# A linear-attention layer on one core: order of the first key bias products, token statistics kept in PSUM, the last query products split around the spread of the key maxima, and a transposition moved into the second state

## The reference

```
xn = layernorm(x) * ln_w + ln_b
q = softmax(xn @ Wq + bq, per head over 64 features)
k = softmax(xn @ Wk + bk + (1 - mask) * -1e6, over the 2048 tokens)
v = (xn @ Wv + bv) * mask
att = sum over tokens of k^T v          (per head, 64 x 64)
y = q @ att
h = layernorm(y) * (1 + scale) + shift  (scale, shift from silu(cond) @ W_emb + b_emb)
out = x + silu(h) @ W_out + b_out
```

## Time and profile before

| | |
|---|---|
| median of three runs | 477.64 us |
| the profiled execution | 476.57 us |
| its span (first to last instruction) | 474.8 us |
| DVE busy | 360.9 us (76%) |
| ACT busy | 263.8 us (56%) |
| POOL busy | 137.6 us (29%) |
| granted clock of PE | 1.00 in nearly all slices |

### The profile page before, as it was taken

How to read it: one execution, slowest core, us unless ns; L and a number is a source line. 1 busy time by engine, 2 the same in 40 slices (tenths; PEclk the granted TensorE clock), 3 DMA queues, 4 the chain that set the end, 5 groups by cost and what they waited for, 6 DMA issues and landing times.

```text
span 474.8 us, 7355 instructions
## 1 busy us (share of the span) xinstructions
PE 458.6 (97%) x2490; PEld 370.4 (78%) x2490; DVE 360.9 (76%) x877; ACT 263.8 (56%) x488; POOL 137.6 (29%) x152
## 2 busy tenths in 40 slices
PE   4999999999999999999999999999999999999997
PEld 2677776886788878888888888888768868888876
DVE  5879976775977956979678667677798628898963
ACT  4633332321887523347555665556789913778882
POOL 0413311121200000104223223333211133676675
PEclk9999999999999999999999999999999999999999
DMA  7966210113132200110213211121322041243222
GB/s 252 365 204 225 110 45 2 45 43 111 50 128 89 90 32 14 46 44 1 72 41 126 92 50 68 66 89 46 133 86 71 0 145 57 90 126 129 100 91 88
DMA packets 23190, 43.50 MB, mean 92 GB/s; under 512 B 1961, under 2 KB 2289, under 8 KB 23153
## 3 DMA queue, kind: packets, MB, share of 16 engines
q1 hardware_dynamic: 22592, 41.98, 25.8%
q10 hardware_dynamic: 560, 1.05, 0.6%
HBM read 34.64 MB, written 8.39 MB: 91 GB/s over the span
## 4 chain that ended last, share of the span: by engine, by line
PE 78%; DVE 10%; issue 4%; POOL 4%; ACT 1%; DMA 1%; POOLq 0%; ACTq 0%; DVEq 0%
PE ps L1211 20%; PE ps L1213 20%; PE ps L1212 20%; PE ps L1216 8%; PE ps L1395 4%; POOL x_in L635 2%; PE ps L1317 2%; DVE ek_lo L850 1%; PE ps L1270 1%; POOL zT_lo L628 1%; DMA y<-in_L_cond_Wk_dram 1%; DVE kf L845 1%; DVE kf L909 1%; DVE res L969 1%; PE ps L1373 1%
## 5 line engine op out<-in xcount | busy, mean ns | idle before, releaser
L619 POOL TENSOR_TENSOR qs<-qs,qmax 128x512 f32<-128x512 f32 x32 | 35.6, 1113 | 172.9 <-DVE qmax L814 172.9
L1211 PE MATMUL ps<-wk_hi,zT_hi 128*128 128x512 f32 x124 | 51.2, 413 | 2.2 <-DVE kf L795 2.2
L1211 PE MATMUL ps<-ek_hi,zm_hi 128*128 128x512 f32 x128 | 50.7, 396 | 2.0 <-DVE ek_lo L850 1.3
L1211 PE MATMUL ps<-wq_hi,zT_hi 128*128 128x512 f32 x128 | 51.7, 404 | 0.0
L1213 PE MATMUL ps<-wq_hi,zT_lo 128*128 128x512 f32 x128 | 50.2, 392 | 0.0
L1212 PE MATMUL ps<-wq_lo,zT_hi 128*128 128x512 f32 x128 | 49.9, 390 | 0.0
L1212 PE MATMUL ps<-ek_lo,zm_hi 128*128 128x512 f32 x128 | 49.9, 390 | 0.0
L1213 PE MATMUL ps<-ek_hi,zm_lo 128*128 128x512 f32 x128 | 49.9, 390 | 0.0
L338 ACT ACTIVATE zT_hi<-ps 128x512 fp32r<-128x512 f32 x32 | 19.1, 596 | 54.6 <-PE ps L1216 54.6
L1213 PE MATMUL ps<-wk_hi,zT_lo 128*128 128x512 f32 x124 | 48.7, 393 | 0.0
L1212 PE MATMUL ps<-wk_lo,zT_hi 128*128 128x512 f32 x124 | 48.4, 390 | 0.0
(11 more groups left out here) (243 smaller groups left out, 1176.8 us busy)
## 6 DMA issues: line engine op xcount, KB each, us to landing
x_in<-in_x_dram SPq DMA_DIRECT2D x35, 512.0 KB, 3.5
res<-in_x_dram SPq DMA_DIRECT2D x24, 256.0 KB, 2.9
out_dram<-res SPq DMA_DIRECT2D x24, 256.0 KB, 2.0
out_dram<-x_in SPq DMA_DIRECT2D x7, 256.0 KB, 2.0
y<-in_L_cond_Wk_dram ACTq DMA_DIRECT2D x2, 512.0 KB, 5.3
kf<-in_L_cond_Wq_dram SPq DMA_DIRECT2D x1, 1024.0 KB, 5.2
eq<-in_L_cond_W_out_dram SPq DMA_DIRECT2D x1, 1024.0 KB, 8.3
wv_mod<-in_L_cond_Wv_dram SPq DMA_DIRECT2D x1, 1024.0 KB, 10.5
```

Of the source, the lines that this page charges most:

```text
L619: pool.tensor_tensor(q_heads, q_heads, qmax[:, n % 2, :].unsqueeze(2).broadcast_to([P, H, DH]), ALU.subtract).then_inc(s["q_shift"], 1)
L1211: pe.matmul(o, a[0], bb[0], start=start, stop=False)
```

## The change

Nothing that is computed changes. The edits:

1. `key_bias(1)` moves from before the first transpositions to after both first key products.
2. On SP, the load of token tiles 4 and 5 goes ahead of the two broadcast bias loads and of the wait for Wq.
3. The statistics' small values of chunks 2, 3 and 4 of the first batch lie in PSUM too (bank `YB`, columns 128 on; chunk 1 stays in `QB`). `y`, `x_r` and `x_shift` stay in SBUF.
4. First state: `product_q(0, 14)` is issued as two blocks, the spread of the maxima, two blocks. DVE's order at that place is rewritten.
5. Second state: `product_q(1, 15)` is issued as one block, the spread, three blocks; `turn_y(HT + 1)` moves from ahead of the state's first product to behind it; on POOL, `add_bias(HT - 1)` goes ahead of `q_shift(1, 15)`.

```diff
-        xst_ps = in_psum(xst, 128)
+        xst_ps = [in_psum(xst, bank, 128) for bank in (QB, YB)]
...
             load_x(0, 0, 2)
+            load_x(0, 0, 4)
             spread(bk, bk_all[:], "bk_in")
             spread(bq, bq_all[:], "bq_in")
             sp.wait_ge(s["wq_in"], 16)
-            load_x(0, 0, 4)
...
                 if t == T - 1:
                     h_low(HT - 1)
+                    add_bias(HT - 1)
                 q_shift(1, t)
-            add_bias(HT - 1)
...
-                if b == 0 and c == 1:
-                    return xst_ps
+                if b == 0 and c:
+
+                    return xst_ps[min(c, 2) - 1]
...
             keys_top(0)
+            k_less_max(0, 0)
+            k_less_max(0, 1)
+            zm_low(0, 0)
             q_add(0, T - 2)
-            k_less_max(0, 0)
-            zm_low(0, 0)
-            k_less_max(0, 1)
+            ek_low(0, 0)
             q_top(0, T - 2)
-            ek_low(0, 0)
-            q_add(0, T - 1)
             zm_low(0, 1)
             ek_low(0, 1)
+            q_add(0, T - 1)
...
-            def product_q(b, n):
+            def product_q(b, n, blocks=range(NB)):
...
-                last.then_inc(s["q_ps"], 1)
+                if NB - 1 in blocks:
+                    last.then_inc(s["q_ps"], 1)
...
             key_bias(0)
-            key_bias(1)
             turn_z(0, 0)
             turn_z(0, 1)
             product_k(0, 0)
             product_k(0, 1)
             pe.wait_ge(s["vec_in"], 5 * 16)
             turn(ps[:, YB + 1, 0:ROWS - FIRST], vec_rows).then_inc(s["vec_ps"], 1)
+            key_bias(1)
...
-            product_q(0, T - 2)
+            product_q(0, T - 2, range(2))
             spread_kmax(0)
+            product_q(0, T - 2, range(2, NB))
...
             turn_kmax(1)
             turn_y(HT)
+            product_q(1, T - 1, range(1))
             spread_kmax(1)
-            product_q(1, T - 1)
+            product_q(1, T - 1, range(1, NB))
             product_out(HT - 1)
-            turn_y(HT + 1)
             for n in range(T):
                 product_g(1, n)
+                if n == 0:
+                    turn_y(HT + 1)
```

More of the change, by code:

```diff
@@ L127, in cond_linear_attention, with in_psum @@
         xst, yst = stat_tiles("xst"), [stat_tiles("yst0"), stat_tiles("yst1")]
-        def in_psum(st, at):
-            mv = ps[:, QB, at:at + 2 * NT].rearrange("p (t k) -> p t k", k=2)
-            v, bits, a, b = (ps[:, QB, at + 2 * NT + NT * k:at + 3 * NT + NT * k] for k in range(4))
+        def in_psum(st, bank, at):
+            mv = ps[:, bank, at:at + 2 * NT].rearrange("p (t k) -> p t k", k=2)
+            v, bits, a, b = (ps[:, bank, at + 2 * NT + NT * k:at + 3 * NT + NT * k] for k in range(4))
             return {"raw": st["raw"], "mv": mv, "v": v, "bits": bits.bitcast(U32), "y": st["y"], "a": a, "b": b}
-        yst_ps = [in_psum(yst[k], 64 * k) for k in range(2)]
-        xst_ps = in_psum(xst, 128)
+        yst_ps = [in_psum(yst[k], QB, 64 * k) for k in range(2)]
+        xst_ps = [in_psum(xst, bank, 128) for bank in (QB, YB)]
         x_r, x_shift = sb("x_r", [P, T]), sb("x_shift", [P, T])
@@ L1261, in product_q @@
                     pe.wait_ge(s["x_norm"], 2)
-                for f in range(NB):
+                for f in blocks:
                     if m == 0:
```

## The result

The changed kernel took 473.05 us (median of four runs, 472.80 to 474.07), the kernel before 477.38 in the same comparison (four runs, 477.07 to 477.81): a ratio of 0.9913, 95% interval 0.9895 to 0.9931. The forecast was 472.8. The profiled executions are 473.26 against 476.57, spans 471.5 against 474.8, so 3.3 us less by the profiles and 4.3 by the medians. Single runs of one kernel differ: over all comparisons of this document the kernel before took from 475.99 to 479.03. What can be followed from row to row is the profile's 3.3.

A forecast was written before the change was run, and what follows sets the result against it. PE was taken as the bound, busy 458.6 of 474.8 us, leaving 16.2 us idle to win from. Terms 0.1 + 1.9 + 0.9 + 1.9 = 4.8 us gave 477.64 - 4.8 = 472.8, own range 471.8 to 473.8, 8-in-10 range 471.1 to 475.4.

The forecast's parts named there:

- All four places: Where PE stands still: first 21 us, 46 to 48 us, start of the first state, start of the second.
- The three terms behind the start: Gains forecast for chunk 2's statistics (1.9 us), the first state (0.9) and the second state (1.9).
- The start: Up to the first query product: turns 1.1 us earlier, moved passes cost 1.0 later; net gain 0.1 us.
- the rival of the slow pace: At the start, PE's slow pace lasts longer: 4.8 - 2.0 = 2.8 us gained, 474.8; chance 8%.
- The earlier load: Tiles 4 and 5 before two bias loads: statistics end by 19.7 instead of 21.01, leaving PE's own queue as limit.
- The statistics: Chunk 2, near 41 to 48 us: two tiny DVE instructions no longer wait out POOL; 1.9 us gained.
- The first state: At its start: earlier spread and subtraction bring tile 0's ek_lo before the queries end; 0.9 us gained.
- The second state: At its start: the turn waits for nothing and DVE's output tile comes 2.1 us earlier; 1.9 us gained.
- The rival of the statistics not getting free of POOL: Chunk 2's statistics stay held because y and x_r stay in SBUF: 2.9 us gained, 474.7; chance 6%.
- that of the starts of the states giving nothing: At both states, shifted POOL operations hold the low parts; 0.1 + 1.9 is left, 475.6; chance 12%.
- The slower one: At both states' starts POOL holds DVE for its operations' full length, adding 6.1 us: 481.7; chance 4%.
- all the idle time goes: At all four places: 0.9, 1.9, 1.2 and 2.4, together 6.4 us gained, 471.2; chance 13%.

The follow-up runs named there:

- e8_semb: Changed kernel with DVE's two small embedding-condition instructions (semb_t) one tile later, behind tile 4's key and query sums; 0.9913 against the kernel before.
- e5_keybias_only: Kernel before with key_bias(1) moved behind the first two key products and nothing else; 1.0003 against the kernel before.
- e4_keybias_back: Changed kernel with key_bias(1) put back ahead of the first transpositions, all else as changed; 0.9915 against the kernel before.
- e1_stats: Kernel before with only the small statistics values of chunks 2 to 4 put in PSUM; 0.9968 against the kernel before.
- e2_state0: Kernel before with only the first state's edits: product_q(0, 14) in two parts around the spread, DVE's order rewritten; 0.9994 against the kernel before.
- e3_state1: Kernel before with only the second state's edits: last query product split, turn_y(13) behind the first state product, POOL's bias addition moved; 0.9966 against the kernel before.
- e11_state1_no_bias: Kernel before with the second state's PE edits, but POOL's bias addition left behind its subtraction; 1.0004 against the kernel before.
- e7_order: Changed kernel with DVE's second query addition (tile 15) ahead of the low part of tile 1's exponentials; 0.9906 against the kernel before.
- e6_warm: Changed kernel with 18 unused transpositions of the identity on PE while it waits for its first data; 0.9913 against the kernel before.

## Why the prediction was right, term by term

The forecast of 472.8 lies 0.25 from the median and inside its own range. All four places were the right ones and the untouched stretches stayed within 0.03 us. Of the stalls named for removal, the 0.63 and the 0.3 and 0.91 at the states went, and the 1.22 of the key sum shrank to 0.27.

That the sum came so close is in part luck, because errors cancel. The three terms behind the start were forecast at 4.7 and brought 3.49 in the trace, 1.2 too much. The medians differ by 4.33 all the same, so about 0.8 must have come from the start, where the forecast had 0.1. The pair of profiled executions doesn't show it (-0.21), but the other runs do, by an estimate: take from the time of each run the 1.79 us around the span and what its kernel's profile has from the first query product to the end. Left is the time to the first query product. It is 22.06 us on average (standard error 0.07) in the 127 runs of the six programs without the earlier load of tiles 4 and 5, and 21.34 (0.16) in the 22 runs of the four programs that have it and no warm-up.

- *The start*, 0.1 forecast, -0.21 measured. The step that failed is the pace. ACT's split came 1.11 earlier, as worked out (9.83 against 10.94), and the moved passes cost 0.86 later (2.84 for six against 1.98 for four), less than the 1.0 charged. That would be 0.25 won. But the first key product, at the lower level until about 13, gave back 0.45: the second one starts at 14.48 against 15.14, only 0.66 earlier. 1.11 - 0.45 - 0.86 = -0.20, the measured -0.21 up to rounding. This is the rival of the slow pace, which was given 8% at a cost of up to 2.0; here it cost 0.45, enough to eat the gain. It is not a fixed price of the edit: with the same start and no gap ahead of the turns PE rose near 10.6 in `e8_semb`. `e5_keybias_only` (1.0003) and, more weakly, `e4_keybias_back` (0.9915) say that the edit is worth nothing that the timing can tell. The page of the Trainium skill cited for that rival, "TensorE: Matmul & The Clock Gate", Part 1, had the clock rise only after sustained activity. The traces agree as far as they go: in all thirteen the first pass over Wk was slow and PE was at work when its pace rose. They don't tell how much work is enough.
- *The earlier load*, costed at nothing, since without it the statistics ended "exactly when PE is ready". That held for the one execution that was profiled. The first query product waits for `x_shift` in four of the six profiles without the load (0.45, 0.24, 0.40 and 0.45 us in `e1_stats`, `e2_state0`, `e3_state1` and `e11_state1_no_bias`) and in none of the seven with it; in the changed kernel the statistics end at 18.96, 2.3 before that product. By the estimate above the load is worth about 0.7 us, the term that the sum left out. By itself it wasn't run, so this is likely and not shown.
- *The statistics*, 1.9 forecast, 1.44 measured, 1.45 alone. The rule by which it was argued held: one input in PSUM is enough. What the sum left out is the next instruction with two inputs in SBUF: `semb_t` at 43.48 used to run after POOL was done, and now runs under it: 0.60 where 0.17 is usual, 0.43 given back. `e8_semb`, which moves it away, has 1.96 there.
- *The first state*, 0.9 forecast, 0.37 measured, 0.33 alone. The cost was named ("POOL's shift of tile 14 now falls on two DVE instructions") but not charged: `ek_low(0, 1)` took 1.53 for 0.68 and held the query addition and all of DVE's work behind it. The low part of tile 2, which was to come 1.2 to 1.8 earlier, ends only 0.37 earlier, counted from the last key product. `e7_order` shortens that `ek_low` to 0.93, puts the addition ahead of it, and wins 0.96 in all.
- *The second state*, 1.9 forecast, 1.68 measured, 1.70 alone. The output tile on DVE did come 2.16 earlier, counted from the transpositions of the maxima (2.1 forecast), and the low part behind it lost 0.44 under POOL's shift (1.12 for 0.68), where 0.2 had been taken off; what is left, 1.7, goes on unchanged to the fourth product. The masked tile's 0.92 had slack. What the prediction had wrong is the share of the parts: it gave the turn alone 0.9 as its lower bound. `e11_state1_no_bias` shows 0.0 for turn and split without POOL's new order.

The rival of the statistics not getting free of POOL is refuted by `e1_stats`, and that of the starts of the states giving nothing by `e3_state1` and the rows of `e2_state0`. The slower one is refuted too: DVE is held by POOL at both states, but for 0.85, 0.39 and 0.44 us in new places, not 6.1. That all the idle time goes is refuted by the stalls that are left, 0.27, 0.28, 0.22 and 1.11.

## What to carry to other kernels

When a stall under another engine goes, the sum should go on to the next instruction of the same kind: here the one that moved into the place of a removed collision took back 0.5 us at the statistics, 0.6 at the first state and 0.4 at the second. Where two waits end at the same resource, a release of one is worth nothing until the other goes too; here one line on POOL decided over 1.7 us that a bigger edit on PE seemed to bring. Work of PE moved out of its slow first microseconds is paid for later (0.86 here), and where a gap opened in its place, PE also came to its upper pace late. And a wait that just isn't there in the one execution that was profiled can be there in most others: the load that was costed at nothing is the example.

## What the runs showed of the hardware that was not expected

- The landing of the first half of Wk lay anywhere from 5.77 to 8.06 us in the thirteen profiled executions, and the first query product came 13.7 to 15.8 us behind it, at 20.23 to 23.10. From there to the end executions hardly differ: 453.71 us in both kernels with the old program there (before and `e5_keybias_only`), and 450.20, 450.01 and 450.24 in three with the new one (the changed kernel, `e4_keybias_back`, `e6_warm`).
- PE's pace rose at another time in each execution, with the same instructions ahead of it: in the five with the old start (before, `e1_stats`, `e2_state0`, `e3_state1`, `e11_state1_no_bias`) near 10.5, 10.4, 11.2, 13.0 and 12.7 us. With one key bias product moved away it rose near 10.6 and 12.9 where PE worked on without a gap (`e8_semb`, `e7_order`), and near 13.0 and 14.4 where it had a gap of 0.87 or 0.51 ahead of the turns, although Wk had landed earliest there (5.77 and 6.23, in the changed kernel and `e5_keybias_only`). That the gap is the cause is likely and not shown.
- Eighteen transpositions ahead of the first pass, 0.21 apart, never reached the upper pace. Behind an idle time of 0.48 the next two passes took 1.61, behind 0.83 they took 2.05; four behind 1.99 took 3.65, where four at the upper level take 1.98 and four without any warm-up took 3.48 to 3.75.
- POOL's work also holds a TENSOR_SCALAR with a single SBUF tile as input: 1.04 for 0.17 at 16 elements, 0.92 for 0.53 at 512. And it goes the other way: POOL's own operation took 1.49 for 1.27 and 1.42 for 1.04 where it began while such an instruction of DVE was running (the masked tile from 330.54 to 331.34, and `zm_lo` from 119.02 to 119.70, in the changed kernel).
- A tiny instruction with a PSUM input took 0.17 and one with SBUF inputs 0.16. From start to start, the last six steps of the chain take 1.18 us before (all in SBUF) and 1.21 after. A fixed price that differs by the memory doesn't show at this size, nor the 0.65 that the prediction had weighed.
